# Swapping the bodies of TensorE's two branches in the second stage of a Mamba-mixer and MLP kernel

## What is computed

```python
x = x + mixer(layernorm(x))      # W_in, causal conv of 4 taps, a selective scan over 64 heads with
                                 # a state of 128, gate, RMS norm, W_out
x = x + mlp(layernorm(x))

def mlp(x):                      # xf: 2048 tokens x 512
    g = xf @ gate_w.T * gate_s   # gate_w, up_w: 1408 x 512; entries are -1, 0 or 1
    u = xf @ up_w.T * up_s
    return (silu(g) * u) @ down_w.T * down_s   # down_w: 512 x 1408; entries are -1, 0 or 1
```

## Time and profile before

| | |
|---|---|
| runs shown | 816.15, 816.83, 817.84 us; median 816.83 |
| the profiled execution: its own time | 815.7 us |
| its span in the trace | 813.6 us |
| mean granted clock of TensorE | 0.965 of full |
| busy: PE, PEld, DVE, ACT, POOL | 92%, 76%, 63%, 62%, 37% of the span |
| second stage | from about 543 us to the end |

### The profile page before, as it was taken

The page is one execution under the profiler, slowest core; times in us unless marked ns, Lnnn a source line. Parts: engine busy times, 40 slices in busy tenths (PEclk is TensorE's granted clock), DMA queues, the critical chain, the costliest instruction groups (busy, mean ns, idle before and its releaser), DMA issues. The chain is left out here.

```text
span 813.6 us, 20282 instructions
## 1 busy us (share of the span) xinstructions
PE 749.9 (92%) x8464; PEld 615.7 (76%) x8464; DVE 515.2 (63%) x839; ACT 505.4 (62%) x963; POOL 297.6 (37%) x245
## 2 busy tenths in 40 slices
PE   5879999999999999999999995639979999999997
PEld 5857878878878878878878873427868887887886
DVE  6878967967967967967967957646522532632431
ACT  6989788798788788798798786024511321321330
POOL 2255187177187177177177173040011001001002
PEclk9979999999999999999999998669999999999999
DMA  9822533633733523433532536920003003102002
GB/s 305 212 78 79 111 85 96 121 82 84 136 80 105 115 79 106 115 82 103 116 88 71 115 86 210 361 71 2 27 29 128 1 14 102 40 0 82 22 1 78
DMA packets 39195, 77.67 MB, mean 95 GB/s; under 512 B 9408, under 2 KB 15040, under 8 KB 39104
## 3 DMA queue, kind: packets, MB, share of 16 engines
q1 hardware_dynamic: 38784, 75.84, 34.2%
q10 hardware_dynamic: 320, 0.52, 0.3%
HBM read 67.43 MB, written 8.92 MB: 94 GB/s over the span
## 5 line engine op out<-in xcount | busy, mean ns | idle before, releaser
L411 POOL TENSOR_TENSOR ring<-tokd,ring 128x1024 f32<-128x1024 f32 x64 | 122.0, 1921 | 188.1 <-ACT tokd L576 127.5
L1066 PE MATMUL ps_proj<-xn_hi,win_hi 128*128 128x256 f32 x608 | 178.8, 294 | 1.5 <-DVE xn_lo L770 1.5
L1067 PE MATMUL ps_proj<-xn_lo,win_hi 128*128 128x256 f32 x608 | 172.6, 284 | 0.0
L1068 PE MATMUL ps_proj<-xn_hi,win_lo 128*128 128x256 f32 x608 | 172.0, 283 | 0.0
L1066 PEld LDWEIGHTS ps_proj<-xn_hi,win_hi 128*128 128x128 f32 x608 | 116.3, 191 | 15.6 <-issue 13.0
L1067 PEld LDWEIGHTS ps_proj<-xn_lo,win_hi 128*128 128x128 f32 x608 | 116.6, 192 | 0.3
L1068 PEld LDWEIGHTS ps_proj<-xn_hi,win_lo 128*128 128x128 f32 x608 | 116.6, 192 | 0.0
L801 DVE SCALAR_TENSOR_TENSOR cx<-cin,consts,cx 128x256 f32<-128x256 f32 x240 | 96.3, 478 | 0.0
L1369 POOL TENSOR_TENSOR res<-res,hidden 128x512 f32<-128x512 f32 x16 | 20.5, 1282 | 188.2 <-DVE hidden L1444 188.2
L1401 ACT ACTIVATE silu_g<-pb,scales 128x512 f32<-128x512 f32 x44 | 30.3, 688 | 94.4 <-PE pb L1513 94.3
L1513 PE MATMUL pb<-x1n_hi,wg_hi 128*128 128x512 f32 x176 | 70.4, 400 | 13.3 <-issue 13.3
(11 more groups left out here) (148 smaller groups left out, 1506.2 us busy)
## 6 DMA issues: line engine op xcount, KB each, us to landing
ring<-cum_dram SPq DMA_DIRECT2D x128, 256.0 KB, 4.9
xin<-x SPq DMA_DIRECT2D x8, 512.0 KB, 4.0
res<-x SPq DMA_DIRECT2D x32, 128.0 KB, 2.6
x_in_sb<-x_dram SPq DMA_DIRECT2D x4, 1024.0 KB, 6.0
res<-x_dram SPq DMA_DIRECT2D x16, 256.0 KB, 2.7
out<-res SPq DMA_DIRECT2D x16, 256.0 KB, 2.0
x_dram<-res SPq DMA_DIRECT2D x28, 128.0 KB, 2.4
wg<-gate_w SPq DMA_DIRECT2D x4, 704.0 KB, 9.8
```

What stands on the lines that cost most here:

```text
L411: pool.tensor_tensor(ring[:, g, :, :], own, ring[:, g, :, :], ALU.subtract).then_inc(diffed, 1)
L1066: pe.matmul(out, win_hi[:, k, cols], xn_hi[:, k, :], start=(k == 0), stop=False)
L1067: pe.matmul(out, win_hi[:, k, cols], xn_lo[:, k, :], start=False, stop=False)
L1068: made = pe.matmul(out, win_lo[:, k, cols], xn_hi[:, k, :], start=False, stop=(k == KT - 1))
```

## The change

Each condition is turned round and the two bodies change places. What is executed for a given flag stays the same.

```diff
-            with pe.If(pe.value_load(hand.low_any[:, 0:1].bitcast(I32)) != 0):
+            with pe.If(pe.value_load(hand.low_any[:, 0:1].bitcast(I32)) == 0):
+                gate_up(0, True, True)
+            with pe.Else():
                 gate_up(0, False, True)
-            with pe.Else():
-                gate_up(0, True, True)
             pe.wait_ge(hand.low_any_made, 2)
             pe.wait_ge(down_hi_made, MT)
 
-            with pe.If(pe.value_load(hand.low_any[:, 1:2].bitcast(I32)) != 0):
+            with pe.If(pe.value_load(hand.low_any[:, 1:2].bitcast(I32)) == 0):
+                rest(True)
+            with pe.Else():
                 rest(False)
-            with pe.Else():
-                rest(True)
```

## The result

The changed kernel takes 806.62 us (median of 4 runs, 805.59 to 808.60) against 816.49 us for the kernel before (4 runs, 815.90 to 817.84): a ratio of 0.988 with a 95% interval of 0.9855 to 0.9904, or 9.9 us (7.8 to 11.8). The forecast was 807.5 us. In a second group of runs it was 807.88 against 818.21 us, ratio 0.9862 (0.9842 to 0.9883).

What follows compares the result with a forecast made beforehand. It took TensorE to bound the second stage, stalled by two taken far branches; 4.36 - 0.44 + 0 + 3.58 + 1.87 = 9.37 us off the median 816.83 gave 807.5 us, range 806.1 to 811.0 us.

Steps and rivals of the forecast that it cites:

- Part 1, the first branch: At L1563, ahead of the first gate/up matmul: not taken, it costs 0.083 instead of 4.441 us, gaining 4.36 us.
- The clock behind the restart: At the first gate/up matmuls: an earlier restart may lengthen the stretch at granted 0.50, costing 0.44 us.
- the upper bound of 4.71 us: Longest slow-clock stretch assumed after TensorE's restart at the first gate/up block; it would cost 0.88 us more.
- Part 2, the exit jump: End of the first exact body: a new jump of 3.663 us, hidden under queued matmuls, so it costs 0.
- the prediction's bound of 0.83 us: Cost of the first body's exit jump if it takes 4.441 us and outlasts its cover.
- Part 3, the second branch: At L1570, ahead of the first down matmul: not taken, it gains 3.58 us; the hole shrinks from 3.8 to 0.2.
- The h_lo that the waits named: Ahead of the first down matmul: h_lo does not bind, since only the 21st matmul of the down tile reads it.
- the 1.87 us for the clock: First two down tiles: with the hole goes the clock at 0.50 behind it, gaining 1.87 us; lower bound nothing.
- Part 4, the last jump: End of the second body: the exit jump hides behind down's tail, VectorE, POOL and the store, so it costs 0.
- the signs named: Signs included an exit-jump record at L1565 or close by, and the 13.3 us "issue" wait falling to 8.9.

Runs made afterwards that it cites:

- e2: The kernel before with only the second branch (L1570) turned round; 812.79 against 818.5 us, ratio 0.9920.
- e11: The kernel before with the plain float32 body skipped by the first branch cut to 8 of 11 tiles; one run, 820.13 us against a median of 817.5.
- e12: The changed kernel plus 31 unread matmuls ending TensorE's first stage and 7 at the start of the second; 805.75 us, ratio to the kernel before 0.9849.
- e3: The changed kernel with TensorE's sequencer waiting for its last gate/up matmul ahead of the first exit jump; 814.31 us, ratio to the kernel before 0.9940.
- e1: The kernel before with only the first branch (L1563) turned round; 814.17 against 818.5 us, ratio 0.9941.
- e6: The changed kernel plus 28 unread matmuls at the end of TensorE's first stage; 807.28 us, ratio to the kernel before 0.9865.
- e4: The changed kernel without value loads, branches and fallback bodies; 806.96 us, ratio to the kernel before 0.9861.
- e7: The changed kernel with TensorE's sequencer waiting for the last down product ahead of the second exit jump; 807.38 us, beside 807.88 for the changed kernel.

## Why the prediction was right

**Part 1, the first branch.** Forecast 4.36 us, measured 4.35 (5.17 to 0.82 from load to matmul). The matmul waited for nothing else of weight; the releaser named now, wu_hi of tile 0, was written 0.40 us ahead of it.

**The clock behind the restart.** Forecast -0.44 us as the middle of 0 and -0.88; measured -0.09. The slow stretch was 3.08 us, near the lower bound. That the loss was near nothing is luck: the upper bound of 4.71 us was too tight, since in e2 the stretch lasted 6.06 us and in e11 5.83, and one like e2's would have cost 1.5 us. Where the rise falls differs from run to run: in the traces of the changed kernel and those built on it (e12 apart, where the clock did not fall), 3.1 to 4.2 us after the restart.

**Part 2, the exit jump.** Forecast 3.66 us long and hidden; measured 3.41 us and hidden, with TensorE busy throughout. e3 shows that the cover is what makes it free. The zero had little room, as the prediction's bound of 0.83 us said: the jump is free up to 3.56 us, and the jumps of e1 (3.90 us) and e6 (3.81 us) came out by 0.33 and 0.25 us. The DMA share, by which 3.66 us was chosen, does not settle a jump's length: the changed kernel's second exit jump took 3.63 us at a share of 0.35, and e12's took 4.99 at 0.37 (at the end of the program, where it cost nothing).

**Part 3, the second branch.** Forecast 3.58 us, measured 3.56. The h_lo that the waits named was not what bound: the hole closed with h_lo at its old place relative to the block. (The prediction has the 21st matmul read it; by the kernel the 22nd does, and the wait for it stands ahead of the 21st, so the sum is the same.) Of the 1.87 us for the clock, 1.59 came. The term was mis-sized by 0.28 us: I had put all of 11.85 - 9.98 down to the slow stretch, but that stretch explains only 3.41 x 0.47 = 1.6 us. The rest stays where the queue has just run dry (10.26 in the changed kernel and 10.24 in e2, against 9.98 in e4).

**Part 4, the last jump.** Forecast 0; e7 shows 0 even with the jump's start held back until the array is done.

The sum was 9.37 us and the trace has 9.41. So close a fit is luck in part: two errors of about 0.3 us (0.35 for the clock behind the restart, 0.28 for the clock behind the hole) cancel, and two traces of the changed kernel differ by 0.17 us from load to end (260.13 and 260.30). Of the signs named, two were off in form only: the exit jump's record stands under the line of its own `If` (L1563), and the wait of 9.0 us is put down to wu_hi and not to "issue".

## What to carry to other kernels

Ask for branch lines by name: a hole that the waits put down to "issue", or to something long done, may be a taken branch to far code, and here each cost 3.4 to 4.4 us, the second one another 1.6 us of clock. Put the body that is executed directly behind the branch, and see that the jump out of it falls where the engine still has some 4 us of work queued and nothing behind the jump is needed sooner; or keep the skipped body short (here 320 instructions were near enough, 512 were not). After such a fix, look at how long the engine has idled ahead of its restart, since the slow matmuls behind it are the next 1 to 1.5 us.

## What the runs showed of the hardware that was not expected

The price of a taken branch is nearly a step: 0.231, 0.361, 4.398 and 4.441 us for 64, 320, 512 and 704 skipped instructions. The jump out of a body costs as much as a taken branch (14 exit jumps in the traces of this study: thirteen of 3.3 to 3.9 us, one of 4.99; 8 taken far branches of 3.4 to 4.4 us), over the first body as over the far longer second one, and keeps its length whether the array runs meanwhile (3.41 us in the changed kernel) or stands (3.59 us in e3). The part that varies is mostly the wait for the packet to start: about 2.0 us at L1563, where the DMA engines are busy at a share of 0.70 to 0.78 (4.32, 4.40 and 4.44 us in all), 0.9 to 1.6 us in the others but one (2.6 us in the jump of 4.99). The loop's body of some 580 instructions, more than two packets, was passed a second time (680.25 to 744.18 us in the trace of before) without a packet on q8: backwards more is kept than is fetched ahead. The first 44 down matmuls are 0.28 us slower straight after a value load and an untaken branch than behind a full queue, though the hole itself is only 0.04 us; the first seven or eight start up to 0.236 instead of 0.227 us apart, the second 0.31 us after the first. Why is left open.
